# Latent attention of a decoder kernel: absorbed rank weights by three products per head pair, with the moved rows made by transfers on chip

## The chip, the cores and the metric

One NeuronCore of a Trainium2 chip runs the whole program; the other cores are idle. The metric is the device time of one execution in microseconds (us), the median of several runs. The engines are TensorE (PE in the rows; PEld is its weight load), VectorE (DVE), ScalarE (ACT), GpSimd (POOL) and SyncE (SP), which issues most of the transfers (DMAs); ScalarE issues some too. Each engine works through its own instructions in order, and they wait for one another by semaphores.

## The reference

Two decoder layers on x of 4 x 256 tokens by 256, all in float32: attention with low-rank updates, latent cross attention, a quantised feed forward, attention with position bias, grouped cross attention, and a mixture of experts. The change is in the latent attention:

```python
q_hk = (hidden_q @ Wq.T).reshape(B, S, H, K)         
q_big = einsum('bshk,hkq->bshq', q_hk, w_kc_q)          # 192 per head
q_big = q_big * cos + rotate_half(q_big) * sin
kv_r = rope(kv_c)                                       # context, 64 wide
q_r = einsum('bshq,hqr->bhsr', q_big, W_qr)             # rank 64
k_r = einsum('bld,hdr->bhlr', kv_r, W_kr)
attn = softmax(einsum('bhsr,bhlr->bhsl', q_r, k_r))
ctx_lat = einsum('bhsd,hkd->bhsk', einsum('bhsl,bld->bhsd', attn, kv_r), w_kc_kv)
x = x + ctx_lat.reshape(B, S, H * K) @ Wo.T
```

`rotate_half` takes the two halves (96 each) of a head's 192 columns, swaps them and changes one's sign.

## The kernel before

`build_program` runs the stages one after another; `mla_stage` is the latent attention. It works through 8 pairs of heads p; each head has 192 query columns, so a pair has 384, three tiles of 128: tile 0 is head 0's first 128, tile 1 holds head 0's last 64 and head 1's first 64 (the shared tile), tile 2 is head 1's last 128. Tokens are worked in two halves of 512.

Instead of making k_r, the kernel absorbs both rank weights into one matrix per head, W_qr times W_kr transposed (192 x 64), so that the queries come out 64 wide and meet the rotated context directly. The queries are multiplied by the cosine and the sine table; the swap of halves is done in the weights: for the sine product, the absorbed matrix is needed with its 192 rows rolled by 96. So a pair needs the absorbed weights in two row orders. For the shared tile they are needed per head, cosine's 64 rows and sine's 64 rows stacked in one matrix of 128 rows.

One pair passes through these steps, named by the functions that issue them:

- `load_k` (L1027) brings pair p's two rank weights from memory: `wkr_in` and `wr_in`; `load_a` and `load_n` bring the others. SyncE issues them a pair ahead, behind a wait for `turned`.
- `turn(p)` (L1495): TensorE transposes `wr_in` (three tiles) and `wkr_in` into bank 5. It waits for `w_k`, the landing of `load_k`.
- `turned_weights(p)` (L1370): ScalarE copies them out, in five activations. Three write `wrT`, which has six slots of 128 columns: besides the three tiles also the rolled row orders. Two write `wkrT`, with each head's block beside zeros which GpSimd has put there (L1175).
- `absorb(p, bank)` (L1506): TensorE makes six products of 128x64, three in the cosine order and three in the sine order.
- `absorbed_weights(p, bank)` (L1225): VectorE copies the six (384 columns) to `wr`, and counts `wr_done`.
- `packed(p, k)` (L1518), k = 0 to 5: the query products, six products of 512 columns each, for half k // 3 and one tile; `rotate` on VectorE multiplies them by the tables into `qcs`.
- `scored_shared` and `scored_own` (L1540, L1552): the absorbed weights times `qcs`, per half; the first needs `wr_done`. ScalarE and VectorE split the result into a high part and a rest (`query_high`, `query_rest`), and SyncE copies the high part to `q2` (`copy_queries`).
- `scores(p, k)`, k = 0 to 7; `maximum`, `denominators`, `logarithms`, `shifts`; `shift_transpose`, `shift_rows` and `send_shifts`, a small transfer of the softmax's shifts to `q2` which `scores_t` (the transposed scores) waits for; `exponentials`; `product`; `context_high` and `context_rest`; `project` and `add`.

The order on each engine is written out by hand. TensorE, per pair: packed 2, `turn(p + 1)`, packed 3, shared products of half 0, packed 4, output weight, own products of half 0, packed 5, `fold(p + 1)`, shared products of half 1, scores 0 to 3, own products of half 1, `absorb(p + 1)`, score 4, the shifts' transpose, scores 5 to 7, transposed scores 0 and 1, packed 0 of the next pair, products, and so on; the last pair's `project` steps lie between the next pair's packed groups. VectorE's `absorbed_weights(p + 1)` stands between `query_rest(p, 1, 1)` and `maximum(p, 4)`. Score 4 waits for `query_rest(p, 1, 0)`, score 5 for `query_rest(p, 1, 1)`.

Before the pairs, TensorE does `fold(0)`, `turn(0)`, two turns of x, `absorb(0)`, two more turns of x, packed 0 and 1 of pair 0 and the transposes of the context. Packed 0 waits there for `wr_done`, since the six products lie in its bank. SyncE issues four loads of the context, and then, pair by pair:

```python
for p in range(PAIRS):
    if p + 1 < PAIRS:
        sp.wait_ge(turned.sem, turned.at(p + 1))
        c.mla.load_k(sp, p + 1)
        sp.wait_ge(folded.sem, p + 1)
        c.mla.load_a(sp, p + 1)
    ...
    sp.wait_ge(mt.sem, 2 * p + 1)
    send_shifts(sp, 0, 1)
```

Of the kernel before, what the change touches and what calls it, by code (L numbers as in the profile page):

```python
# [15 lines left out]
F32 = mybir.dt.float32  # L16
# [3 lines left out]
ALU = mybir.AluOpType  # L20
# [3 lines left out]
P = 128  # L24
# [1017 lines left out]
def mla_stage(c):  # L1042
    nc, io = c.nc, c.io
    with ExitStack() as st:
# [9 lines left out]
        wrT, wkrT = sb("wrT", [P, 6, P]), sb("wkrT", [P, 2 * CTX])  # L1054
        wr = sb("wr", [P, 2, 2, 3, R])
# [25 lines left out]
        zeroed, tern = c.counter("at_m5"), c.counter("at_m4")  # L1081
# [16 lines left out]
        EV = 5  # L1098
        TILE_ORDER = (1, 0, 2)
        WR_SLOTS = ((0, 2), (1, 4), (5, 3))  # L1100
# [28 lines left out]
        with nc.Block() as block:  # L1129

            @block.sync
            def _(sp):
# [12 lines left out]

                src = io["ctx"].rearrange("(t p) d -> p t d", p=P)
# [3 lines left out]
                sp.dma_start(tabk, io["rope_k"].rearrange("p k t d -> p k (t d)")).then_inc(ctx_in.sem, 16)  # L1150
                for p in range(PAIRS):
                    if p + 1 < PAIRS:
                        sp.wait_ge(turned.sem, turned.at(p + 1))
# [3 lines that stand above are left out]
                    if p == 0:  # L1157
                        copy_keys()
                    copy_queries(p, 0)
                    if p + 1 < PAIRS:  # L1160
                        sp.wait_ge(n_done.sem, p + 1)
                        c.mla.load_n(sp, p + 1)
                    copy_queries(p, 1)
                    sp.wait_ge(mt.sem, 2 * p + 1)
                    send_shifts(sp, 0, 1)

            @block.gpsimd
            def _(pool):
# [6 lines left out]
                pool.memset(wkrT[:, :], 0.0).then_inc(zeroed.sem, 1)  # L1175
                pool.wait_ge(zeroed.sem, zeroed.at(1))
                pool.memset(kLt[CTX:CTX + 2, :].bitcast(F32), 1.0).then_inc(zeroed.sem, 1)
                pool.wait_ge(zeroed.sem, zeroed.at(2))
# [21 lines left out]
            def _(dve):  # L1200
# [24 lines left out]
                def absorbed_weights(p, bank):  # L1225
                    dve.wait_ge(absorbed.sem, p + 1)
                    dve.tensor_scalar(wr[:, p % 2, :, :, :].rearrange("p j t n -> p (j t n)"),  # L1227
                                      c.ps[:, bank, 0:6 * R], 1.0, None, ALU.mult).then_inc(wr_done.sem, 1)
# [136 lines left out]
            def _(act):  # L1365
# [4 lines left out]
                def turned_weights(p):  # L1370
                    act.wait_ge(turned.sem, turned.at(p + 1))
                    ps = c.ps[:, TURN_BANK, :]
                    dst = wrT[:, :, :].rearrange("p t n -> p (t n)")
                    act.activation(dst.rearrange("p (k n) -> p k n", n=DCQ)[:, 0:4:3, :],
                                   ps[:, 0:2 * DCQ].rearrange("p (h n) -> p h n", h=2), ACT.Copy)\
                        .then_inc(turned_ev.sem, 1)
                    act.activation(dst[:, DCQ:DCQ + 448].rearrange("p (h n) -> p h n", h=2)[:, :, 0:160],
                                   ps[:, 32:352].rearrange("p (h n) -> p h n", h=2), ACT.Copy).then_inc(turned_ev.sem, 1)
                    act.activation(dst[:, 352:416].rearrange("p (h n) -> p h n", h=2),
                                   ps[:, 0:2 * DCQ].rearrange("p (k n) -> p k n", n=32)[:, 0:12:11, :], ACT.Copy)\  # L1380
                        .then_inc(turned_ev.sem, 1)
                    for h in range(2):
                        act.activation(wkrT[rows(h), h * CTX:(h + 1) * CTX], ps[rows(h), 3 * P:3 * P + CTX], ACT.Copy)\
                            .then_inc(turned_ev.sem, 1)
# [62 lines left out]
                act.wait_ge(zeroed.sem, zeroed.at(2))  # L1447
# [34 lines left out]
            def _(pe):  # L1482
# [23 lines left out]
                def absorb(p, bank):  # L1506
                    pe.wait_ge(turned_ev.sem, turned_ev.at(EV * p + EV))
                    if p:
                        pe.wait_ge(mp_lo.sem, p + 1)
                    for j in range(2):  # L1510
                        for tile in range(3):
                            h = (0, j, 1)[tile]
                            mm = pe.matmul(c.ps[:, bank, (3 * j + tile) * R:(3 * j + tile + 1) * R],
                                           wrT[:, WR_SLOTS[tile][j], :], wkrT[:, rows(h)],
                                           start=True, stop=True)
                    mm.then_inc(absorbed.sem, 1)
# [23 lines left out]
                def scored_shared(p, half):  # L1540
                    pe.wait_ge(rope.sem, rotated(p, 3 * half + 1))
                    if half == 0:
                        pe.wait_ge(wr_done.sem, p + 1)
# [4 lines left out]
                    for h in range(2):  # L1548
                        pe.matmul(c.ps[rows(h), 4 + half, :], wr[:, p % 2, h, 1, :], qcs[:, half, 1, h, :],
                                  start=True, stop=False, skip_group_check=True)  # L1550

                def scored_own(p, half):  # L1552
                    pe.wait_ge(rope.sem, rotated(p, 3 * half + 3))
                    for cs in range(2):
                        for h, tile in ((0, 0), (1, 2)):
                            mm = pe.matmul(c.ps[rows(h), 4 + half, :], wr[:, p % 2, cs, tile, :],
# [39 lines left out]
                def scores_t(p, b):  # L1596
# [3 lines left out]
                    if b == 0:  # L1600
                        pe.wait_ge(mt.sem, 2 * p + 1)
                        pe.wait_ge(q_lo.sem, 4 * p + 4)
                        if p == 0:
                            pe.wait_ge(zeroed.sem, zeroed.at(2))
# [113 lines left out]
        for s, n in ((stats_done, TT), (mv_done, TT), (var_done, 2), (std_done, 2), (rstd_done, 2),  # L1718
# [3 lines left out]
                     (zeroed, 2)):  # L1722
# [1535 lines left out]
```

## Time and profile before

| | us |
|---|---|
| median of 3 runs | 812.61 (811.94 to 814.03) |
| profiled execution, its span | 812.5 |

| engine | busy us in the span | share |
|---|---|---|
| PE | 722.5 | 89% |
| DVE | 577.6 | 71% |
| PEld | 462.7 | 57% |
| ACT | 425.3 | 52% |
| POOL | 198.0 | 24% |

The latent attention takes about 111 to 414 us of the span. Busy shares are means over stages with different limits, so each step is read from the timeline of its own stretch. A matmul's end is modelled and overlaps the next one's start; "idle before" is what the engine lay idle ahead of an instruction, and the name behind the arrow is who ended it; "issue" means that nothing in the profile shows the wait. SPq and ACTq rows are a queue's issuing of transfers, not the transfers themselves.

### The profile page before, as it was taken

How to read it: one execution, taken by the hardware profiler on the slowest of the kernel's cores; microseconds unless marked ns; L12 is line 12 of the kernel's file. 1: busy time of each engine (PE TensorE's matmuls, PEld its weight loads, DVE VectorE, ACT ScalarE, POOL GpSimd, SP SyncE). 2: the span in 40 equal slices, each digit the busy share in tenths (PEclk: the TensorE clock that was granted, in tenths of full speed). 3: DMA queues.
4: the chain of work that ended last, by engine and by line, in shares of the span. 5: the costliest groups of instructions: out<-in, count | busy, mean ns of one | idle time of the engine just before them, and what ended most of it. 6: DMA issues, size and time to landing. Idle time of an engine off the chain costs nothing. (4 is left out here: it accounts for less than half of the span.)

```text
span 812.5 us, 13314 instructions
## 1 busy us (share of the span) xinstructions
PE 722.5 (89%) x4826; PEld 462.7 (57%) x4826; DVE 577.6 (71%) x1117; ACT 425.3 (52%) x888; POOL 198.0 (24%) x298
## 2 busy tenths in 40 slices
PE   5999989999999999999757469999589999879997
PEld 3555666666666666666533345666344444368886
DVE  5578678686767667686669854565668999665666
ACT  4557753544636364543649655455366676533332
POOL 2422010303123030303225314120121111352450
PEclk9999999999999999999979679999859999969999
DMA  4725422111202111110153006130010323403111
GB/s 120 194 60 158 148 70 69 48 45 34 76 7 72 30 49 36 42 43 1 27 135 75 9 8 191 45 80 2 21 41 21 81 59 90 120 2 106 54 50 52
DMA packets 49760, 52.24 MB, mean 64 GB/s; under 512 B 10116, under 2 KB 40388, under 8 KB 49588
## 3 DMA queue, kind: packets, MB, share of 16 engines
q1 hardware_dynamic: 49062, 51.06, 23.4%
q8 instruction: 39, 0.64, 0.3%
q10 hardware_dynamic: 634, 0.33, 0.2%
q14 instruction: 25, 0.20, 0.1%
HBM read 26.58 MB, written 2.04 MB: 35 GB/s over the span
## 5 line engine op out<-in xcount | busy, mean ns | idle before, releaser
L427 DVE TENSOR_REDUCE a_nm<-ps 128x2 f32<-128x512 f32 (+1 forms) x112 | 75.3, 688 | 28.4 <-PE ps L723 19.4
L2499 DVE TENSOR_REDUCE x_nm<-ps 128x2 f32<-128x512 f32 x128 | 84.9, 685 | 12.4 <-PE ps L2640 10.1
L2584 ACT ACTIVATE x_pt<-ps 128x1024 f32<-128x1024 f32 x64 | 62.4, 1020 | 34.6 <-PE ps L2668 33.9
L1535 PE MATMUL ps<-m_xp,m_mp 128*128 128x512 f32 x288 | 75.4, 397 | 1.0 <-DVE m_wr L1227 1.0
L1406 ACT ACTIVATE m_junk<-ps,m_nm 128x256 bf16<-128x256 f32 x128 | 58.6, 483 | 25.8 <-DVE m_nm L1244 25.8
L1191 POOL TENSOR_SCALAR fw<-fw,finv 128x256 f32<-128x256 f32 x24 | 11.6, 482 | 223.7 <-PE ps L1613 223.7
L2640 PE MATMUL ps<-kx,a_qs 96*128 96x256 bf16 x256 | 53.1, 296 | 8.2 <-DMA a_qs<-a_ks 6.5
L1535 PEld LDWEIGHTS ps<-m_xp,m_mp 128*128 128x128 f32 x288 | 50.7, 188 | 15.4 <-issue 6.1
L3068 PE MATMUL ps<-x_xp,x_wp 128*128 128x512 f32 x216 | 55.2, 407 | 0.0
L1207 DVE TENSOR_TENSOR m_qcs<-ps,mw_tab 64x512 f32<-64x512 f32 x64 | 44.0, 688 | 7.5 <-PE ps L1535 4.3
L1214 DVE TENSOR_TENSOR m_qcs<-ps,mw_tab 128x512 f32<-128x512 f32 x64 | 41.1, 684 | 7.4 <-PE ps L1535 7.1
L3068 PEld LDWEIGHTS ps<-x_xp,x_wp 128*128 128x128 f32 x216 | 41.2, 196 | 8.6
L2640 PEld LDWEIGHTS ps<-kx,a_qs 96*128 96x128 bf16 x256 | 20.6, 101 | 41.2 <-issue 13.2
L2684 PE MATMUL ps<-x_pt,a_ks 128*32 128x256 f32 x512 | 41.8, 399 | 2.6 <-DVE x_av L2508 2.6
L1244 DVE TENSOR_REDUCE m_nm<-ps 128x2 f32<-128x512 f32 x64 | 39.8, 680 | 1.0 <-PE ps L1574 1.0
L1574 PE MATMUL ps<-m_kHH,m_qs 128*128 128x256 f32 x128 | 33.9, 302 | 6.8 <-DVE m_qs L1237 4.4
L2668 PE MATMUL ps<-a_qs,kx 98*128 98x512 bf16 x128 | 39.6, 392 | 0.0
L1426 ACT ACTIVATE m_pt<-ps 128x1024 f32<-128x1024 f32 x32 | 31.0, 1017 | 14.1 <-PE ps L1613 14.1
L575 ACT ACTIVATE a_pt<-ps 128x1024 f32<-128x1024 f32 x32 | 32.1, 1019 | 10.6 <-PE ps L758 10.6
L575 ACT ACTIVATE fw<-ps 128x1024 f32<-128x1024 f32 (+1 forms) x32 | 25.8, 810 | 22.0 <-PE ps L774 21.9
L1629 PE MATMUL ps<-m_pt,m_kvr 128*64 128x256 f32 x256 | 33.4, 391 | 1.8 <-ACT m_pt L1426 1.4
L1574 PEld LDWEIGHTS ps<-m_kHH,m_qs 128*128 128x128 f32 x128 | 24.9, 194 | 16.2 <-issue 7.3
(306 smaller groups left out, 1673.8 us busy)
## 6 DMA issues: line engine op xcount, KB each, us to landing
a_qs<-a_parts SPq DMA_DIRECT2D x48, 128.0 KB
a_ks<-a_parts SPq DMA_DIRECT2D x48, 128.0 KB
m_q<-m_qs SPq DMA_DIRECT2D x32, 128.0 KB
x_gb<-scr_g SPq DMA_DIRECT2D x8, 512.0 KB, 3.8
fw<-in_f_w SPq DMA_DIRECT2D x12, 256.0 KB
a_qs<-a_ks SPq DMA_DIRECT2D x48, 64.0 KB
mw_wq<-in_m_wq SPq DMA_DIRECT2D x8, 256.0 KB, 2.8
mw_wo<-in_m_wo SPq DMA_DIRECT2D x8, 256.0 KB, 2.8
```

Source lines behind the costliest of these rows:

```text
L427: dve.tensor_reduce(dst, src, AX.X, ALU.max, negate=True).then_inc(mx_done.sem, 1)
L575: act.activation(pt[:, n % 2, kt, 0:banks * BANK], c.ps[:, 2 + 2 * kt:2 + 2 * kt + banks, :].rearrange("p b n -> p (b n)"), ACT.Exp, scale ...
L1207: dve.tensor_tensor(qcs[rows((cs, 1 - cs)[h]), half, 1, h, :].rearrange("p (b q) -> p b q", q=SEQ), c.ps[rows(h), QB_BANKS[k], :].rearrang ...
L1214: dve.tensor_tensor(qcs[:, half, tile, cs, :].rearrange("p (b q) -> p b q", q=SEQ), c.ps[:, QB_BANKS[k], :].rearrange("p (b q) -> p b q", ...
L1406: act.activation(junk[:, n % 4, :], c.ps[:, S_BANKS[k % 4], qt * SEQ:(qt + 1) * SEQ], ACT.Exp, bias=nm[:, k // 4, one], accum_out=den[:, k ...
L1535: mm = pe.matmul(c.ps[:, QB_BANKS[k], :], mp[:, p % 2, w, dt, tile * P:(tile + 1) * P], xp[:, x, dt, half_cols(half)], start=((dt, w, x) = ...
L1574: mm = pe.matmul(c.ps[:, S_BANKS[k % 4], qt * SEQ:(qt + 1) * SEQ], qs[:, h, q0:q0 + P], part[:, seq_cols(b)], start=(low == 0), stop=(low ...
L2499: dve.tensor_reduce(nm[:, n % ITEMS, QT * u:QT * u + QT], c.ps[:, u % 2, :].rearrange("p (t k) -> p t k", t=QT), AX.X, ALU.max, negate=Tru ...
L2584: act.activation(pt[:, n % 2, kt, :], c.ps[:, 2 + 2 * kt:4 + 2 * kt, :].rearrange("p b n -> p (b n)"), ACT.Exp, scale=SCALE).then_inc(exp_ ...
L2640: mm = pe.matmul(c.ps[:, u % 2, qt * SEQ:(qt + 1) * SEQ], queries(slice(0, S_ROWS), n, u).squeeze(1)[:, qt * P:(qt + 1) * P], kx[0:S_ROWS, ...
L2684: mm = pe.matmul(c.ps[rows(h), 6, 0:SEQ], vs[:, QT * b + kt, g, :], pt[:, n % 2, kt, h * SEQ:(h + 1) * SEQ], start=(kt == 0), stop=(kt == ...
L3068: mm = pe.matmul(up_bank(j, half), wp[:, b, w, at:at + EH], xp[:, x, dt, cols(half)], start=((dt, w, x) == terms[0]), stop=((dt, w, x) == ...
```

## The change

The rank weights are absorbed once, in the cosine order only: `wrT` has three tiles, copied in one piece; `wkrT` has 64 columns, copied in one piece, and no zeros (the other head's part is zero in `wr_in` itself). Three products per pair take the place of six, and VectorE copies 192 columns. The rows of the other order, and the stacked rows of the shared tile, are moved from `wr` to a new tile `wm` by ten transfers per pair, of 32 or 64 rows with 256 bytes each, which SyncE issues behind a wait for `wr_done`: for pair 0 ahead of its pair loop, for pair p + 1 at the end of pair p. The shared products wait for the ten transfers (`wm_in`) in place of `wr_done`. GpSimd's memset of `wkrT` goes.

```diff
-        wrT, wkrT = sb("wrT", [P, 6, P]), sb("wkrT", [P, 2 * CTX])
-        wr = sb("wr", [P, 2, 2, 3, R])
+        wrT, wkrT = sb("wrT", [P, 3, P]), sb("wkrT", [P, CTX])
+        wr, wm = sb("wr", [P, 2, 3, R]), sb("wm", [P, 2, 4, R])
...
-        EV = 5
+        EV = 2
         TILE_ORDER = (1, 0, 2)
-        WR_SLOTS = ((0, 2), (1, 4), (5, 3))
+        MOVES = ((0, 0, 0, 96, 32), (0, 32, 1, 0, 64), (0, 96, 0, 0, 32),
+                 (1, 0, 1, 0, 64), (1, 64, 0, 32, 64), (2, 0, 2, 32, 64), (2, 64, 1, 64, 64),
+                 (3, 0, 2, 96, 32), (3, 32, 1, 64, 64), (3, 96, 2, 0, 32))
...
+                def move_weights(p):
+
+                    sp.wait_ge(wr_done.sem, p + 1)
+                    for to, row, tile, first, count in MOVES:
+                        sp.dma_start(wm[row:row + count, p % 2, to, :], wr[first:first + count, p % 2, tile, :])\
+                            .then_inc(wm_in.sem, 16)
+
...
                 sp.dma_start(tabk, io["rope_k"].rearrange("p k t d -> p k (t d)")).then_inc(ctx_in.sem, 16)
+                move_weights(0)
                 for p in range(PAIRS):
...
                     send_shifts(sp, 0, 1)
+                    if p + 1 < PAIRS:
+                        move_weights(p + 1)
...
-                pool.memset(wkrT[:, :], 0.0).then_inc(zeroed.sem, 1)
+                pool.memset(kLt[CTX:CTX + 2, :].bitcast(F32), 1.0).then_inc(zeroed.sem, 1)
                 pool.wait_ge(zeroed.sem, zeroed.at(1))
-                pool.memset(kLt[CTX:CTX + 2, :].bitcast(F32), 1.0).then_inc(zeroed.sem, 1)
-                pool.wait_ge(zeroed.sem, zeroed.at(2))
...
-                    dve.tensor_scalar(wr[:, p % 2, :, :, :].rearrange("p j t n -> p (j t n)"),
-                                      c.ps[:, bank, 0:6 * R], 1.0, None, ALU.mult).then_inc(wr_done.sem, 1)
+                    dve.tensor_scalar(wr[:, p % 2, :, :].rearrange("p t n -> p (t n)"),
+                                      c.ps[:, bank, 0:3 * R], 1.0, None, ALU.mult).then_inc(wr_done.sem, 1)
...
+                    act.activation(wrT[:, :, :].rearrange("p t n -> p (t n)"), c.ps[:, TURN_BANK, 0:3 * P], ACT.Copy)\
                         .then_inc(turned_ev.sem, 1)
...
+                    act.activation(wkrT[:, :], c.ps[:, TURN_BANK, 3 * P:3 * P + CTX], ACT.Copy)\
                         .then_inc(turned_ev.sem, 1)
...
-                    for j in range(2):
-                        for tile in range(3):
-                            h = (0, j, 1)[tile]
-                            mm = pe.matmul(c.ps[:, bank, (3 * j + tile) * R:(3 * j + tile + 1) * R],
-                                           wrT[:, WR_SLOTS[tile][j], :], wkrT[:, rows(h)],
-                                           start=True, stop=True)
+                    for tile in range(3):
+                        mm = pe.matmul(c.ps[:, bank, tile * R:(tile + 1) * R], wrT[:, tile, :], wkrT[:, :],
+                                       start=True, stop=True)
...
                     if half == 0:
-                        pe.wait_ge(wr_done.sem, p + 1)
+                        pe.wait_ge(wm_in.sem, wm_in.at(16 * len(MOVES) * (p + 1)))
...
-                        pe.matmul(c.ps[rows(h), 4 + half, :], wr[:, p % 2, h, 1, :], qcs[:, half, 1, h, :],
+                        pe.matmul(c.ps[rows(h), 4 + half, :], wm[:, p % 2, 1 + h, :], qcs[:, half, 1, h, :],
...
-                            mm = pe.matmul(c.ps[rows(h), 4 + half, :], wr[:, p % 2, cs, tile, :],
+                            w = wm[:, p % 2, 3 * h, :] if cs else wr[:, p % 2, tile, :]
+                            mm = pe.matmul(c.ps[rows(h), 4 + half, :], w,
```

## Rows read from the trace of the kernel before

**Rows 1.** Windows of about a pair: TensorE's busy us come first, its clock after POOL
```profile
126.00:161.00 35.00, 33.47 (x182) 21.32 (x180) 27.10 (x48) 17.76 (x54) 7.23 (x9) 1.00 0.27 68
...
232.00:268.00 36.00, 34.60 (x195) 22.75 (x194) 25.78 (x47) 17.74 (x54) 7.20 (x9) 1.00 0.16 44
```

**Rows 2.** Timeline of TensorE in pair 2: start, duration, engine, line, operation
```profile
213.58 1.55 PE L1513 MATMUL ps<-m_wkrT,m_wrT 128*128 128x64 f32 x12
215.24 0.36 PE L1574 MATMUL ps<-m_kHH,m_qs 128*128 128x256 f32 x1
...
216.69 0.35 PE L1574 MATMUL ps<-m_kHH,m_qs 128*128 128x256 f32 x1 [0.55 <-DVE m_qs L1237]
...
218.72 0.47 PE L1612 MATMUL ps<-m_qs,m_kHH 128*128 128x512 f32 x1 [0.39 <-issue]
...
222.72 2.23 PE L1629 MATMUL ps<-m_pt,m_kvr 128*64 128x256 f32 x16
...
232.82 0.49 PE L1502 MATMUL ps<-ident,mw_wr_in 128*128 128x128 f32 x3
```

**Rows 3.** Timeline of VectorE in the same pair
```profile
204.26 0.41 DVE L1262 TENSOR_TENSOR m_wn<-ps,m_wn 128x256 fp32r<-128x256 f32 x1
...
209.62 0.96 DVE L1222 TENSOR_TENSOR m_mp<-ps,m_mp 128x768 fp32r<-128x768 f32 x1
...
214.41 0.68 DVE L1237 TENSOR_TENSOR m_qs<-ps,m_qs 64x512 fp32r<-64x512 f32 x1
...
216.57 0.56 DVE L1227 TENSOR_SCALAR m_wr<-ps 128x384 f32<-128x384 f32 x1
```

**Rows 4.** Timeline of ScalarE in the same pair
```profile
217.76 0.47 ACT L1406 ACTIVATE m_junk<-ps,m_nm 128x256 bf16<-128x256 f32 x1 [1.32 <-DVE m_nm L1244]
...
221.66 1.92 ACT L1426 ACTIVATE m_pt<-ps 128x1024 f32<-128x1024 f32 x2
...
239.72 0.38 ACT L1388 ACTIVATE m_wn<-ps 128x256 fp32r<-128x256 f32 x1 [4.91 <-PE ps L1593]
```

**Rows 5.** Timeline of all engines at the start of the stage
```profile
115.23 1.00 SPq L1029 DMA_DIRECT2D mw_wr_in<-in_m_wr  x1
...
120.18 0.55 DVE L1227 TENSOR_SCALAR m_wr<-ps 128x384 f32<-128x384 f32 x1
...
122.17 1.30 POOL L1184 TENSOR_TENSOR m_kvr<-m_qcs 128x512 f32<-128x512 f32 x1
...
125.96 0.49 PE L1502 MATMUL ps<-ident,mw_wr_in 128*128 128x128 f32 x3
```

**Rows 6.** Issues by line: ns of one issue, min/median/max, first and last start
```profile
L1136 SPq DMA_DIRECT2D m_q<-m_qs x32: 461/468/511, 133.8 to 395.4; - x32
...
L1126 SPq DMA_DIRECT2D m_q<-m_mT x8: 687/691/692, 144.0 to 396.0; - x8
...
L1024 SPq DMA_DIRECT2D mw_wq<-in_m_wq x8: 429/430/433, 92.9 to 327.4; - x8
```

**Rows 7.** Issues of the keys' load, and the rank load's time from issue to landing
```profile
L1028 SPq DMA_DIRECT2D mw_wkr_in<-in_m_wkr x8: 529/710/734, 93.8 to 326.0; - x8
...
DMA to landing us min/median/max: 2.5/2.6/5.4
```

**Rows 8.** Windows around two falls of TensorE's clock, columns as in rows 1
```profile
392.20:395.70 3.50, 1.69 (x9) 0.62 (x5) 2.48 (x7) 3.09 (x14) 0.00 (x0) 0.98 0.17 37
395.70:399.10 3.40, 2.89 (x13) 2.92 (x14) 2.44 (x4) 2.21 (x10) 0.00 (x0) 0.51 0.18 41
...
473.90:477.50 3.60, 0.00 (x0) 0.00 (x0) 3.02 (x10) 0.00 (x0) 2.65 (x1) 1.00 0.05 1
...
479.30:487.70 8.40, 7.67 (x15) 3.74 (x16) 3.81 (x15) 6.86 (x17) 0.00 (x0) 0.50 0.02 4
```

**Rows 9.** ScalarE's shifts of the second half, and the transposed scores behind them
```profile
223.75 1.28 ACTq L1126 DMA_DIRECT2D m_q<-m_mT  x2
...
226.37 0.39 PE L1612 MATMUL ps<-m_qs,m_kHH 128*128 128x512 f32 x1
```

More of the change, by code:

```diff
@@ L1080, in mla_stage @@
         xp_hi, xp_lo = c.counter("at_in3"), c.counter("at_in4")
-        zeroed, tern = c.counter("at_m5"), c.counter("at_m4")
+        zeroed, tern, wm_in = c.counter("at_m5"), c.counter("at_m4"), c.counter("at_m6")
         w_a, w_k, w_n, tab_in = c.mla.w_a, c.mla.w_k, c.mla.w_n, c.mla.tab_in
@@ L1371, in turned_weights @@
                     act.wait_ge(turned.sem, turned.at(p + 1))
[L1372 to L1375, printed above, removed]
+                    act.activation(wrT[:, :, :].rearrange("p t n -> p (t n)"), c.ps[:, TURN_BANK, 0:3 * P], ACT.Copy)\
                         .then_inc(turned_ev.sem, 1)
[L1377 to L1380, printed above, removed]
+                    act.activation(wkrT[:, :], c.ps[:, TURN_BANK, 3 * P:3 * P + CTX], ACT.Copy)\
                         .then_inc(turned_ev.sem, 1)
-                    for h in range(2):
-                        act.activation(wkrT[rows(h), h * CTX:(h + 1) * CTX], ps[rows(h), 3 * P:3 * P + CTX], ACT.Copy)\
-                            .then_inc(turned_ev.sem, 1)
                 def weight_high(p):
@@ L1446, in _ @@
                 fold_high(0)
-                act.wait_ge(zeroed.sem, zeroed.at(2))
                 turned_weights(0)
@@ L1603, in scores_t @@
                         if p == 0:
-                            pe.wait_ge(zeroed.sem, zeroed.at(2))
+                            pe.wait_ge(zeroed.sem, zeroed.at(1))
                     if b == 1:
@@ L1721, in mla_stage @@
                      (dn, 16 * PAIRS), (ln_done, 2 * PAIRS), (ms, 6 * PAIRS), (wn_lo, PAIRS), (tern, 9 * PAIRS),
-                     (zeroed, 2)):
+                     (zeroed, 1), (wm_in, 16 * len(MOVES) * PAIRS)):
             s.done(n)
```

## The prediction

> **What bounds the kernel now.** I read, in this order: the page's busy shares and slices, the windows of one head pair each, the timelines of TensorE, VectorE, ScalarE and SyncE over one steady pair, and the first 30 us of the latent attention stage. The change touches that stage alone (about 111 to 414 us of the span of 812.5). A pair takes 36 us and TensorE is busy 34.6 of them [rows 1], so TensorE looks like the bound. The timeline says more: inside a pair there is a stretch, from the products that finish the queries' second half to the first context products, where TensorE waits for others. Score 4 starts at 215.24, right after VectorE's query rest, which runs 0.68 from 214.41 and ends at 215.09; the next score starts after an idle 0.55, put down to VectorE; the transposed scores start after 0.39 [rows 2, 3]. There the order is ScalarE's and VectorE's: maxima, eight denominators, a logarithm, exponentials. In pair 0 TensorE has hardly a gap (33.47 busy of 35.00) [rows 1], so there whatever holds it up for long is paid.
>
> **TensorE: three products fewer per pair.** The six products take 1.55 from 213.58 [rows 2]; half is 0.78. But score 4 can't start before 215.09 (the rest) plus some 0.1, and the six end at 215.13. So TensorE would now wait for VectorE where it multiplied: worth 0, in all seven pairs that do it there. If VectorE's query parts were faster, this would be worth up to 0.78 a pair. For pair 0's own weights TensorE next waits for normalised rows, also 0.
>
> **ScalarE: two copies for five.** Two stay, one of 128x384 and one of 128x64. After the five ScalarE idles 4.91 for the output weight [rows 4]. Worth 0.
>
> **VectorE: 192 columns copied, not 384.** The copy takes 0.56; 128x256 takes 0.41 and 128x768 0.96, about 1.07 ns a column, so 192 fewer save 0.2 [rows 3]. The maximum behind it starts 0.2 earlier, and ScalarE, which had waited 1.32 for that maximum, starts its eight denominators 0.2 earlier; they, a logarithm and the exponential at 221.66 run without a pause, and the context products at 222.72 wait for that exponential [rows 2, 4]. TensorE's own queue before those products leaves some 0.1 of that uncertain, because the transposed scores at 218.72 wait for something else, the shifts' transfer. I take 0.17 a pair: 7 x 0.17 = 1.2 gained, between 0.7 and 1.4.
>
> **GpSimd: one memset fewer.** It then waits for normalised rows anyway; its last product starts at 122.17 and ends at 123.47, and the key transposes wait for that. So the 0.2 that VectorE's shorter copy gives the first packed products of pair 0 is stopped there too. Worth 0 [rows 5].
>
> **SyncE: ten transfers per pair, and what they are put ahead of.** In pairs 0 to 6 they follow SyncE's last transfer of the pair: from about 217.2, behind the copy, to 222.3 at 0.51 each (below). Behind them stand the loads for the pair after next, which land by about 227 and are turned at 232.82 [rows 2]; the moved weights are read after that turn. Worth 0, apart from a collision, below.
>
> Before pair 0 it is otherwise. SyncE now waits for the copy of the absorbed weights (VectorE, from 120.18, now 0.35 long, so 120.53), issues ten transfers, and only then loads pair 1's rank weights, which it had issued at 115.23 [rows 5]. Pair 1's turn is the next thing that TensorE does after the third packed group, at 125.96, and TensorE takes its queue in order: packed groups, scores and all stand behind it. How long does one issue take? The nearest row is the on-chip copy of 64 rows of the queries: 468 ns, with 0.04 between two; bounds are 430 (a load of 128 rows) and 691 (the shifts, few rows) [rows 6]. Sum: 120.53 + 0.05 + 10 x 0.51 = 125.7; the keys' load 0.71 + 0.04, so the rank load is issued at 126.45; it lands 2.6 later [rows 7], 129.05, and the turn's products start at about 129.25, where they had started at 125.96. **Cost 3.3**; with 430 it is 2.9, with 691 it is 5.1, and a slower landing (up to 5.4 is seen) would add. Pair 0 has no slack on TensorE to give it back, and all later pairs follow it.
>
> One sentence of the Trainium skill bears on that price: DMA: Bandwidth & Descriptors, section "Why a DMA increments its semaphore by 16 and not by 1", gives 512 sequencer cycles per transfer on earlier generations, and TensorE: Matmul & The Clock Gate, Part 1, a sequencer at 1.2 GHz, which is 0.43 us. The loads' row agrees (430), the on-chip copy's doesn't (468); by the page the forecast would be 815.6.
>
> **The clock in that hole.** TensorE would be idle for 3.3 us at 125.9. In the trace it lay idle from 473.9; the granted clock was 1.00 until 477.5 and 0.50 from there, and the engine then worked through 8.4 us (479.3 to 487.7) at that level, 1.2 GHz. Less idle time did it too: in pair 7 the engine was busy 1.69 of 3.50 from 392.2, and the clock was 0.51 from 395.7 to 399.1 [rows 8]. So I take it that the hole costs a fall. Work of 3.4 us at half rate loses 1.7; 8.4 us would lose 4.1; none loses 0. I take 1.8, nearer the first, since the queue behind the hole is dense as in that stretch.
>
> **Sum**, against the profiled 812.5 (its median of runs is 812.61, so 0.1 is added): +3.3 +1.8 -1.2 = +3.9, **816.4**.
>
> **Rivals.**
> (a) The clock doesn't fall in the hole: 812.6 + 3.3 - 1.2 = 814.7. For it: where a gap lies seems to matter, since after the idle start at 473.9 it took 3.6 us to fall. Against: pair 7, with less idle. 20%.
> (b) The four loads for the next pair but one, moved some 5 us back by the transfers, now fly when ScalarE sends the shifts of the second half. Those are issued from 223.75 for 1.28, and the transposed scores start at 226.37 with no wait, 2.0 after the second issue; so there may be little slack [rows 9]. Loads beside them could add 0.3, in six pairs: +1.8, 818.2. Landing times of the rank load itself go from 2.5 to 5.4 with what else is in flight [rows 7]. 18%. 
> (c) Not slower: the six products are on the path after all. Place: ahead of score 4. Price: 0.78 x 7 = 5.4 gained, 816.4 - 5.4 = 811.0. It decides if score 4 waits for TensorE's queue and not for the query rest, that is if the rest is done before 214.4. Against: it ends at 215.09 and score 4 follows it by 0.15. 7%.
> (d) The new 0.8 us gap ahead of score 4, beside those of 0.55 and 0.39, lets the clock fall in the steady pairs as in pair 7. There 3.4 us went at 0.51, which costs up to 1.7; in half of the seven pairs that is +6.0, 822.4. Against: the three gaps sum to 1.7 over more than 4 us, where pair 7 had 1.81 idle in 3.50. 7%.
> Some 3% is left for what I don't see; the forecast has 45%.
>
> **Range and chances.** Low end: (a) with issue at its cheapest and all of VectorE's gain, 812.6 + 2.9 - 1.4 = 814.1, less 0.2 for runs. High end: issue at 691 and 2.6 for the clock, 812.6 + 5.1 + 2.6 - 0.7 = 819.6, which also holds (b); (c), (d) and part of the last 3% lie outside, under 2 in 10. 0.3% is 2.4 us, about what a measurement of this kernel can tell from no change, so slower means above 815.0: nearly all of the forecast, all of (b) and (d), a quarter of (a): 0.77. Same: the rest of (a) and a little of (c): 0.17. Faster: most of (c): 0.06.
>
> **What would show it.** In the profile of the changed kernel: TensorE idle for about 3.3 us ahead of pair 1's turn, released by the rank load; SyncE's ten issues in a row at about 0.5 each from 120.6; granted clock 0.5 soon after; in a steady pair a wait of about 0.8 ahead of score 4 put down to VectorE's query rest, the copy of the absorbed weights at 0.35, a pair shorter by 0.1 to 0.2. Wrong if pair 1's turn isn't held up, if an issue takes well under 0.4, or if steady pairs are shorter by 0.7 or longer than before.

## The result and the profile after

The changed kernel took 819.05 us in the median of four runs (817.93 to 820.97), beside 813.31 for the kernel before in the same session: ratio 1.0073, 95% interval 1.0053 to 1.0092. Measured once more in six runs it gave 820.19 beside 813.41, ratio 1.0073 (1.0052 to 1.0095). So it is slower, by 5.7 to 6.8 us. The profiled execution has a span of 819.2 against 812.5.

The page of the changed kernel, its head (busy us, share of the span, instructions; then the DMA packets):

```profile
span 819.2 us, 13272 instructions
PE 722.8 (88%) x4778; PEld 463.2 (57%) x4778; DVE 577.5 (70%) x1117; ACT 420.3 (51%) x864; POOL 197.9 (24%) x297
...
DMA packets 55137, 53.30 MB, mean 65 GB/s; under 512 B 15492, under 2 KB 45764, under 8 KB 54964
```

TensorE executes 48 matmul instructions fewer and is busy no less (722.5 before). ScalarE is busy 5.0 less; copy_ahead (experiment 4) has ScalarE's two copies too, and its pairs take what they took before, so nothing came of it.

**Where the time is.** A good ruler is VectorE's copy of the absorbed weights, which starts once in each pair. Its starts in the changed kernel (the first to the fourth, and the eighth), then the second, third, and eighth of the kernel before (the first and fourth stand in [rows 5] and [rows 3]):

```profile
120.05 0.34 DVE L1237 TENSOR_SCALAR m_wr<-ps 128x192 f32<-128x192 f32 x1
150.72 0.36 DVE L1237 TENSOR_SCALAR m_wr<-ps 128x192 f32<-128x192 f32 x1
186.80 0.36 DVE L1237 TENSOR_SCALAR m_wr<-ps 128x192 f32<-128x192 f32 x1
223.23 0.36 DVE L1237 TENSOR_SCALAR m_wr<-ps 128x192 f32<-128x192 f32 x1
...
367.44 0.36 DVE L1237 TENSOR_SCALAR m_wr<-ps 128x192 f32<-128x192 f32 x1
```

```profile
144.09 0.56 DVE L1227 TENSOR_SCALAR m_wr<-ps 128x384 f32<-128x384 f32 x1
180.33 0.56 DVE L1227 TENSOR_SCALAR m_wr<-ps 128x384 f32<-128x384 f32 x1
361.60 0.56 DVE L1227 TENSOR_SCALAR m_wr<-ps 128x384 f32<-128x384 f32 x1
```

First interval: 30.67 against 23.91, so +6.76. The six steady ones: 216.72 against 217.51 together, so -0.79; five of them are 36.03 to 36.08 where before they were 36.24 to 36.27, and one is 36.43. Nearly the whole loss is made between the start of the stage and the second pair's weights. Ahead of the first copy the two traces differ by 0.13, behind the eighth by 0.86.

Timeline of SyncE, then of TensorE, at the start of the stage in the changed kernel (start, duration, engine, line; in brackets idle time and what ended it):

```profile
120.42 6.31 SPq L1152 DMA_DIRECT2D m_wm<-m_wr  x10
126.77 0.59 SPq L1028 DMA_DIRECT2D mw_wkr_in<-in_m_wkr  x1
127.41 0.59 SPq L1029 DMA_DIRECT2D mw_wr_in<-in_m_wr  x1
```

```profile
120.54 3.88 PE L1532 MATMUL ps<-m_xp,m_mp 128*128 128x512 f32 x12 [0.24 <-DVE m_wr L1237]
...
125.04 1.63 PE L1532 MATMUL ps<-m_xp,m_mp 128*128 128x512 f32 x6
130.13 0.90 PE L1502 MATMUL ps<-ident,mw_wr_in 128*128 128x128 f32 x3 [3.45 <-DMA mw_wr_in<-in_m_wr]
130.96 0.37 PE L1503 MATMUL ps<-ident,mw_wkr_in 64*128 64x64 f32 x1
131.26 2.93 PE L1532 MATMUL ps<-m_xp,m_mp 128*128 128x512 f32 x6
```

And windows of the same stretch (busy us of PE, PEld, DVE, ACT, POOL, then TensorE's clock, DMA share, GB/s):

```profile
119.00:123.00 4.00, 3.76 (x12) 2.91 (x13) 2.66 (x5) 2.48 (x3) 3.81 (x3) 0.57 0.04 9
123.00:127.00 4.00, 3.68 (x21) 2.76 (x19) 3.68 (x6) 1.02 (x1) 0.00 (x1) 1.00 0.11 24
127.00:129.00 2.00, 0.00 (x0) 0.00 (x0) 2.00 (x3) 0.00 (x0) 0.00 (x0) 1.00 0.24 47
129.00:136.00 7.00, 5.87 (x14) 2.80 (x14) 2.39 (x5) 0.60 (x2) 0.00 (x0) 0.52 0.69 201
```

The ten moves go first, the rank load behind them is issued at 127.41 and lands for the turn at 130.13; TensorE stands idle for 3.45 with everything queued behind the turn, and then works 7 us at a clock of 0.52 (1.2 GHz of 2.4): six packed products take 2.93, which take 1.67 or less at the full clock.

From the first copy to the turn it is 10.08 us, against 5.78 before [rows 5]: +4.30. From the turn to the second copy it is 20.59 against 18.13: +2.46. That is the 6.76.

### The profile page after: what moved, and what is told of

The parts are those of the page before. It is cut to its first block and busy times, and to the rows that moved or that the text cites. A ratio compares the mean times of both kernels' runs of the same rounds, so it can differ in the third digit from the quotient of the medians.

```text
span 819.2 us, 13272 instructions
## 1 busy us (share of the span) xinstructions
PE 722.8 (88%) x4778; PEld 463.2 (57%) x4778; DVE 577.5 (70%) x1117; ACT 420.3 (51%) x864; POOL 197.9 (24%) x297
## 5 line engine op out<-in xcount | busy, mean ns | idle before, releaser
L1532 PE MATMUL ps<-m_xp,m_mp 128*128 128x512 f32 x288 | 77.5, 406 | 0.2 <-DVE m_wr L1237 0.2
L1532 PEld LDWEIGHTS ps<-m_xp,m_mp 128*128 128x128 f32 x288 | 52.4, 193 | 15.7 <-issue 4.8
```

Of the source, the lines that this page charges most:

```text
L1532: mm = pe.matmul(c.ps[:, QB_BANKS[k], :], mp[:, p % 2, w, dt, tile * P:(tile + 1) * P], xp[:, x, dt, half_cols(half)], start=((dt, w, x) = ...
```

## The experiments

All of them are timed beside the kernel before, whose median was 813.2 to 813.4 each time. "Interval" below is from one start of the copy of the absorbed weights to the next.

**1. The place of the rank load.** In loads_first SyncE issues pair 1's four loads ahead of pair 0's moves:

```
+                sp.wait_ge(turned.sem, turned.at(1))
+                c.mla.load_k(sp, 1)
+                sp.wait_ge(folded.sem, 1)
+                c.mla.load_a(sp, 1)
                 move_weights(0)
                 for p in range(PAIRS):
-                    if p + 1 < PAIRS:
+                    if 0 < p and p + 1 < PAIRS:
```

> The changed kernel with one difference: SyncE issues pair 1's four loads ahead of pair 0's ten transfers, as soon as pair 0's turn is done. Theory (the rank load stood behind the transfers, and TensorE, in order, behind the load): pair 1's turn starts at about 125.5 to 126.5, not 130.1; the shared products may now wait up to 1 for the last transfer; from VectorE's first copy of absorbed weights to its second 24 to 25 us, not 30.7; the time is 812 to 813.5. Rival (the ten transfers as such, or the shared products' new wait for them, cost the time, wherever they are issued): first interval over 28, time 817 or more.

Measured: 813.6 us (10 runs, 811.69 to 816.51), ratio 1.0007 (0.9991 to 1.0022). TensorE at the start of the stage:

```profile
119.23 5.05 PE L1536 MATMUL ps<-m_xp,m_mp 128*128 128x512 f32 x12 [0.23 <-DVE m_wr L1241]
...
126.40 0.49 PE L1506 MATMUL ps<-ident,mw_wr_in 128*128 128x128 f32 x3
126.82 0.27 PE L1507 MATMUL ps<-ident,mw_wkr_in 64*128 64x64 f32 x1
127.02 1.65 PE L1536 MATMUL ps<-m_xp,m_mp 128*128 128x512 f32 x6
128.60 1.08 PE L1550 MATMUL ps<-m_qcs,m_wm 128*64 128x512 f32 x4
```

The turn waits for nothing, nor do the products at 128.60 that read the moved weights, whose last move was issued 3 us before. One reordering gives back the whole loss, so the place of the load is its cause, and the ten moves as such cost nothing here. But the first interval is 25.54, not below the 23.91 of before: the first twelve packed products took 5.05, where they take 2.97 to 2.99 at the full clock. That is taken up in 3. The six later intervals are 36.24, 36.37, 36.06, 36.42, 36.15 and 36.06; the clock fell in the fourth of them only.

five_five puts pair 1's four loads (the four lines added above) between the first five moves and the last five:

```
+                move_weights(0, MOVES[:5])
...
+                move_weights(0, MOVES[5:])
```

> The changed kernel with five of pair 0's ten transfers issued ahead of pair 1's four loads and five behind them. Theory (the hole is the queue's issue time, 0.63 us a transfer): the rank load is issued 3.1 us earlier, at about 124.3, lands at about 127, TensorE waits 0.5 to 1.0 for it, the clock does not fall there, the first interval is about 25, and the time is 813 to 814.5. Rival (a fixed cost of waiting for the copied weights, whatever the count): a wait of TensorE of over 2.5 remains and the time stays above 816.

Measured: 814.74 us (10 runs), ratio 1.0012 (1.0000 to 1.0024), first interval 25.78. The rank load was issued at 122.28, the turn ran at 125.70, with no wait (I had expected 0.5 to 1.0; the low clock ahead of it, with twelve products in 5.00, brought TensorE there later):

```profile
125.70 0.49 PE L1507 MATMUL ps<-ident,mw_wr_in 128*128 128x128 f32 x3
```

Half the moves ahead of the load cost 1.1 at most (814.74 against 813.6, and the intervals of the two ratios overlap), all ten cost the turn 4.3: the price is not so much per move, it begins where the load's landing passes TensorE's arrival at the turn.

**2. The clock behind the hole.** hole_filled keeps the changed kernel's order and gives TensorE 14 unused products to make where it would stand idle; hole_half gives it 8; their results are overwritten.

```
+                    if p == 0:
+                        pe.wait_ge(xp_lo.sem, xp_lo.at(4))
+                        for _ in range(14):
+                            pe.matmul(c.ps[:, 4, :], mp[:, 0, 0, 0, 0:P], xp[:, 0, 0, half_cols(0)],
+                                      start=True, stop=True)
                     if p + 1 < PAIRS:
                         turn(p + 1)
```

> The changed kernel with 14 products more (128x512, their result is not used) on TensorE ahead of pair 1's turn, where it lay idle for the rank load. Theory (behind the hole the granted clock was 0.50 for 6.7 us, and that costs time on top of the wait): the turn still starts at about 130, the clock stays 1.00 from 126 to 136, the first interval is about 28.3, not 30.7, and the time falls by 2 to 2.5. Rival (what follows the hole is limited by VectorE or by transfers, and the clock is only a sign): the clock stays 1.00 but the first interval stays above 30 and the time within 0.5 of 819.

> hole_filled once more, for a second profile: its first one showed a first interval of 28.48 with the clock at 1.00 behind the hole, yet its timed runs lie at 821. Theory: in some executions the low clock that begins at about 117 lasts into the 14 added products; at half rate they take 6 us instead of 3.3 and reach past the landing of the load, so that the span is 819 and the first interval about 31. Rival: the profile is as the first one (span about 816), and the timed runs are later for another reason.

> The changed kernel with 8 products more ahead of pair 1's turn instead of 14: at half rate they take 3.4 us and still end before the load lands. Theory (the low clock behind the hole costs about 2.2): where the clock stays up the first interval is about 28.5, where it falls 30.7; the turn starts at 130 either way; median 816.5 to 819, below the changed kernel's 819.05, never clearly above it. Rival (the clock behind the hole costs nothing): median 819 to 820.

TensorE in hole_filled, and its window behind the hole:

```profile
126.23 3.34 PE L1677 MATMUL ps<-m_xp,m_mp 128*128 128x512 f32 x14
129.41 0.49 PE L1502 MATMUL ps<-ident,mw_wr_in 128*128 128x128 f32 x3
...
130.03 1.66 PE L1532 MATMUL ps<-m_xp,m_mp 128*128 128x512 f32 x6
```

```profile
129.00:136.00 7.00, 7.00 (x33) 3.74 (x33) 4.15 (x7) 0.99 (x3) 0.00 (x0) 1.00 0.57 149
```

And in hole_half, where 1.60 of idle time was left:

```profile
126.29 2.00 PE L1677 MATMUL ps<-m_xp,m_mp 128*128 128x512 f32 x8
129.89 0.55 PE L1502 MATMUL ps<-ident,mw_wr_in 128*128 128x128 f32 x3 [1.60 <-DMA mw_wr_in<-in_m_wr]
```

The first interval came to 28.48, 28.71 and 27.97, with the clock at 1.00 behind the hole in all three. From the turn to the second copy they need 17.93, 17.91 and 17.94, alike; the kernel before needs 18.13, the changed one 20.59. So in the profiles the wait alone is worth 4.3 and the clock 2.7. The 0.2 between 18.13 and 17.93 is not VectorE's shorter copy, which lies ahead of the turn. It goes with a late turn: loads_first and loads_ahead (5), whose turn comes 7.7 behind the first copy, need 17.88 and 17.89, while the kernels of 3 and 4 with the turn 5.6 to 5.8 behind it need 18.06 to 18.13, with the short copy or the long one. Only five_five (7.6 and 18.19) doesn't fit. So pair 0 gives back 0.2 of the hole; what work it is that has got ahead by then isn't shown. The profile of hole_filled_2 is also where I was wrong: I had expected the added products to run at half rate; they ran at the full one.

The medians follow this badly. hole_filled took 821.0 (818.02, 821.0, 821.01, 821.68; the profiled one is the fastest; ratio 1.0096, 1.0071 to 1.0120), where I had expected 2 to 2.5 less than 819.05; hole_filled_2 took 820.28 in its one run, hole_half 818.63 (four runs, ratio 1.0062, 1.0039 to 1.0085), where 819.05 less 2.7 would have been 816.4. Two losses can be named. The 14 products hold up the turn themselves: it comes 10.55 and 10.80 behind the first copy, not 10.08 (with 8 products 10.03). And in hole_filled_2 the second interval is 37.15, with a low clock from 148 to 151. These don't make up the difference, and the rest isn't explained. To see whether the changed kernel's fall itself is there only in some runs, it ran once more:

> The changed kernel once more, unedited. Its first profile was that of its slowest run (820.97), with TensorE's clock at 0.5 for 6.7 us behind the hole and a first interval of 30.67; the kernels with products added in the hole had 28.0 to 28.7 at full clock, but were not faster in the median (818.6 and 821.0 against 819.05). Theory (the fall behind the hole is there in every run): first interval 30.5 to 30.8 again, median 819 to 820. Rival (it comes in some runs only, and the first profile caught one of them): first interval near 28.3 with the clock at 1.00 behind the hole, or a median under 818.5.

First interval 30.51, median 820.19, and the low clock lay in the same places: from 118, 128, 186, 367 and 401, where the first profile has 119, 129, 187, 368 and 402. The fall behind the hole was in both profiles of the changed kernel. But that falls keep their places in every run isn't shown: hole_filled and hole_filled_2 are one kernel, and the low clock begins at 116, 256 and 399 in the one, at 117, 147, 185, 366 and 400 in the other. (The Trainium skill, TensorE: Matmul & The Clock Gate, "What's actually happening", says of a kernel's start that the number of products at the low clock varies from run to run. The two profiles of hole_filled vary in that way, though in the middle of a kernel; the two of the changed kernel don't.) What keeping the fall away is worth in the time stays open: 2.7 in three profiles of the stretch, nothing that the medians of four runs can show.

**3. Three products fewer.** six_products is loads_first with each of the three products made twice, so that TensorE has its six again (the second three are never read); VectorE copies 192 columns. six_in_pair_0 does so for pair 0 alone (its range is 6 for pair 0 and 3 for the others).

```
-                    for tile in range(3):
+                    for tile in range(6):
-                        mm = pe.matmul(c.ps[:, bank, tile * R:(tile + 1) * R], wrT[:, tile, :], wkrT[:, :],
+                        mm = pe.matmul(c.ps[:, bank, tile * R:(tile + 1) * R], wrT[:, tile % 3, :], wkrT[:, :],
```

> loads_first with the three products of each pair made twice (six, the second three into columns that nobody reads); VectorE still copies 192 columns. Theory (TensorE's three products fewer are worth nothing, because score 4 waits for VectorE's query rest): score 4 starts as long after the own products as in loads_first, a steady pair takes 36.05 in both, and the time is that of loads_first within 0.5, or below it if the filled gap spares falls of the clock. Rival (the products are on the path): 0.7 to 0.8 a pair more, 36.8, and 5 us more in all.

> loads_first with the three products of pair 0's weights made twice, the other pairs' once. Theory (with three products fewer between the two halves of x TensorE idles longer there, 1.15 instead of 0.48, and the clock falls at about 117, which costs about 1.6 at the packed groups): no low clock before 125, first interval 23.6 to 23.9 as in six_products; steady pairs still show one to three falls; time 1 to 1.5 below loads_first's 813.6. Rival (that fall comes with the place of the loads, not with the products): low clock at 117 to 124 as before, first interval 25.5.

six_products: 812.67 us (10 runs), ratio 0.9989 (0.9975 to 1.0003), intervals 23.66 and then 36.06 to 36.12. six_in_pair_0: 814.2 (10 runs), ratio 1.0012 (0.9995 to 1.0029), intervals 23.66, then 36.05 to 36.11 with two of 36.41 and 36.45. The steady pair is 36.05 to 36.1 with six products, and three don't shorten it: the six steady intervals together are 216.53 in six_products and 216.80 in six_ahead (5), and 216.72 to 217.43 in the kernels with three, hole_filled_2 with its 218.21 left aside. So the three products fewer gain nothing there. And the three that are missing in pair 0 do harm. Timeline of TensorE ahead of the first packed products and windows of that stretch, first in loads_first:

```profile
114.78 0.78 PE L1515 MATMUL ps<-m_wkrT,m_wrT 128*128 128x64 f32 x6
116.71 2.30 PE L1656 MATMUL ps<-ident,xn 128*128 128x128 f32 x8 [1.15 <-DVE xn L1306]
```

```profile
117.00:124.00 7.00, 6.77 (x20) 5.09 (x20) 5.04 (x10) 2.48 (x3) 3.82 (x3) 0.52 0.12 35
```

then in six_in_pair_0:

```profile
115.26 1.45 PE L1515 MATMUL ps<-m_wkrT,m_wrT 128*128 128x64 f32 x12
117.19 1.73 PE L1656 MATMUL ps<-ident,xn 128*128 128x128 f32 x8 [0.48 <-DVE xn L1306]
119.72 2.97 PE L1536 MATMUL ps<-m_xp,m_mp 128*128 128x512 f32 x12 [0.79 <-DVE m_wr L1241]
```

```profile
117.00:124.00 7.00, 6.02 (x31) 4.61 (x32) 5.42 (x12) 2.77 (x4) 3.83 (x3) 1.00 0.14 45
```

With 0.67 us less work TensorE stands idle for 1.15, not 0.48, and then works 7 us at 0.52 of its clock; the first interval is 25.54 instead of 23.66. In the changed kernel the same fall begins at 119 (twelve products in 3.88 instead of 2.97), but it is hidden there, since the turn waits for the load, which doesn't hang on TensorE. In the time this 1.9 too is not to be seen: I had expected 1 to 1.5 less than loads_first, and six_in_pair_0 is no faster in the median (814.2 and 813.6, the intervals overlap). Its profile has four stretches of 3.4 at the low clock in the stage (from 179, 288, 360, 394), that of loads_first has two behind the start (253, 396); and from the eighth copy to the end of the span the one needs 451.3, the other 448.8. That the clock takes at one place what it gives at another isn't shown by this.

One thing is shown by all the profiles together. Nine of them have three products in the steady pairs (the changed kernel's two, loads_first, five_five, hole_filled's two, hole_half, six_in_pair_0, loads_ahead), and in each the clock falls one to three times behind the second to eighth copy, 18 falls in all, every one beginning within 1 us of the start of a copy: right behind the new wait of 0.8 ahead of score 4 and the 0.55 ahead of score 5 that was there before. The five with six products (before, six_products, six_and_copy, copy_ahead, six_ahead) have none in that stretch. So it is the three missing products that let the clock fall in steady pairs too. Such an interval takes 36.37 to 36.45, once 37.15 (the second interval of hole_filled_2). In the changed kernel:

```profile
187.00:191.00 4.00, 4.00 (x17) 3.67 (x18) 2.83 (x5) 3.21 (x15) 0.00 (x0) 0.57 0.21 47
```

**4. VectorE's copy, and a collision.** six_and_copy is six_products with VectorE copying 384 columns again (the last 192 are never read), meant to measure the copy alone.

```
-                    dve.tensor_scalar(wr[:, p % 2, 0:3, :].rearrange("p t n -> p (t n)"),
-                                      c.ps[:, bank, 0:3 * R], 1.0, None, ALU.mult).then_inc(wr_done.sem, 1)
+                    dve.tensor_scalar(wr[:, p % 2, 0:6, :].rearrange("p t n -> p (t n)"),
+                                      c.ps[:, bank, 0:6 * R], 1.0, None, ALU.mult).then_inc(wr_done.sem, 1)
```

> six_products with VectorE copying all 384 columns: apart from the transfers it does the kernel before's work. Theory (VectorE's shorter copy is what shortens a pair, by 0.17 to 0.2): steady pairs 36.25 instead of 36.06 to 36.12, time 1.0 to 1.4 above six_products, that is level with the kernel before, so that the ten transfers of the steady pairs cost nothing. Rival (the transfers cost something that the shorter copy has hidden): pairs above 36.3 and time above 814.5.

Measured: 817.02 us (6 runs), ratio 1.0047 (1.0029 to 1.0065), intervals 23.88, then 37.12, 37.24, 37.29, 37.28, 36.27, 37.02: about a whole microsecond more in five pairs of six, for 0.2 of VectorE, with no low clock in them. Timeline of a steady pair:

```profile
224.48 0.59 SPq L1028 DMA_DIRECT2D mw_wkr_in<-in_m_wkr  x1
224.52 1.32 ACTq L1128 DMA_DIRECT2D m_q<-m_mT  x2
225.12 0.59 SPq L1029 DMA_DIRECT2D mw_wr_in<-in_m_wr  x1
...
228.10 0.47 PE L1614 MATMUL ps<-m_qs,m_kHH 128*128 128x512 f32 x1 [0.78 <-issue]
```

ScalarE's two shifts leave at the very moment of SyncE's loads, and the transposed scores, which wait for the shifts, start late. In six_products the loads are issued at 222.07 and the shifts at 221.91, just ahead of them, and there is no such wait. Nor is there in the one pair of six_and_copy that takes 36.27: there the shifts go out at 299.10, the loads at 299.25, and the scores start at 301.72, 2.62 behind the shifts. If that is the cause, the loads have only to be moved. copy_ahead is the same kernel, with each pair's four loads ahead of its moves:

```
                     send_shifts(sp, 0, 1)
+                    if p + 2 < PAIRS:
+                        sp.wait_ge(turned.sem, turned.at(p + 2))
+                        c.mla.load_k(sp, p + 2)
+                        sp.wait_ge(folded.sem, p + 2)
+                        c.mla.load_a(sp, p + 2)
                     if p + 1 < PAIRS:
                         move_weights(p + 1)
```

> This is six_and_copy (three products made twice, copy of 384 columns) with one thing moved: in every pair SyncE issues the four loads for the pair after next ahead of the ten moves, not behind them. Theory (the loads' transfers, issued at the same moment as ScalarE's shifts, held these back): the transposed scores start with no wait of 0.8, the steady pairs go from 37.1-37.3 back to 36.2-36.3, the span from 814.8 to about 808 to 809.5 if no clock fall comes, 811 in the median. Rival (VectorE's longer copy is what costs 1.0 per pair): pairs stay at 37.1-37.3, the time at 817.

Measured: 813.45 us (12 runs), ratio 1.0004 (0.9994 to 1.0014), intervals 23.85, then 36.24 to 36.27 all six. The same place:

```profile
223.29 1.28 ACTq L1128 DMA_DIRECT2D m_q<-m_mT  x2
...
225.91 0.40 PE L1614 MATMUL ps<-m_qs,m_kHH 128*128 128x512 f32 x1
```

From the shifts' issue to the scores: 3.58 us beside the loads, 2.62 without them. So the collision is real and costs 0.8 to 1.0 a pair; and moves that are being issued at that moment, as here (ten from 219.10 for 6.5), cost nothing in this kernel. copy_ahead and six_products together also price VectorE's 192 columns: 36.25 with them (as in the kernel before), 36.05 to 36.1 without; and from the first copy to the turn 5.78 with them, 5.58 without. The time fell by 3.6, less than the 6 that I had written: the eight copies lie closer by 4.7 (246.1 to 241.4), and behind the eighth 1.0 was lost again.

**5. The change without its faults.** loads_ahead is the changed kernel with the order of copy_ahead, six_ahead the same with each product made twice.

> The changed kernel with the loads of every pair ahead of its moves (the best form of the change that keeps three products). Theory: as loads_first, first interval 25.5, steady pairs 36.05 or 36.4 where the clock falls in one, 813.6 in the median, level with before. Rival (rival b of the prediction was at work in small in the changed kernel): pairs 0.1 to 0.3 shorter than in loads_first, time 812 or less.

> six_products (three products made twice, copy of 192 columns) with the loads ahead of the moves in every pair. Theory: no collision was left to remove there (its transposed scores waited 0.2 at most), so pairs stay at 36.05 to 36.1, and the time within 1 of 812.7. Rival (the loads behind the moves cost something in every pair that I don't see): pairs fall to 35.9 or less, time under 811.7.

loads_ahead: 813.23 us (12 runs), ratio 1.0002 (0.9992 to 1.0013), intervals 25.62, then 36.08 to 36.41. six_ahead: 812.56 (12 runs), ratio 0.9985 (0.9974 to 0.9996), intervals 23.66, then 36.07 to 36.11 with one of 36.36 (no fall; the transposed scores came 2.82 behind the shifts there, and why isn't shown). So the best of the forms tried here is level with the kernel before, or 0.15% faster (six_ahead; six_products alone is not clear of no change) if TensorE is kept as busy as it was: about what VectorE's shorter copies give, 7 x 0.17 = 1.2 by the prediction, of which 0.8 is seen. Neither order differs from its partner in 1 and 3 (813.6 and 812.67), so in the changed kernel no collision was at work.

## Why the prediction was right, and where its sizes were off

It said 816.4, slower, in 813.9 to 819.6; it was 819.05, and 820.19 when it was measured again, which is 0.6 above the range. The mechanism and its place were right (1). The two larger terms were too small, by 1.0 and 0.9, and a fall in a steady pair (+0.4, rival (d)) was left out of the sum; so the range held by little.

- **The wait for the rank load, +3.3.** Measured +4.30. The failing step is the price of an issue: I took 0.51 from the copy of 64 rows of the queries [rows 6], with the 0.04 between two, and bounded it by 691 ns. The moves' rows are 575, 595 and 1141 ns (least, median, most, 80 of them) with 0.04 between two, 0.63 together:

```profile
L1152 SPq DMA_DIRECT2D m_wm<-m_wr x80: 575/595/1141, 120.4 to 373.9; - x80
```

  Ten take 6.35 instead of 5.1. The landing (130.13 - 127.41 = 2.72) was as taken. The truth lay about halfway between the two rows; I had chosen near the cheaper end. (The Trainium skill's 512 cycles per transfer, DMA: Bandwidth & Descriptors, section "Why a DMA increments its semaphore by 16 and not by 1", misses these rows by more: 0.43 for 0.595. The loads of `wq` agree with it, 430; the rank load, also of 128 rows, took 579 to 825 in the changed kernel.) Two of the sums beside the forecast leave out the 0.04 between two issues: with it, 691 ns gives 5.5 and not 5.1, and the top of the range 820.0; and the time by the skill's figure is 816.0 and not 815.6.
- **The clock behind the hole, +1.8.** It fell, where I said. It cost 2.7 in the profiles (2), with 0.2 given back by the late turn. It stayed low for 6.7 us, nearer the longer of my two examples [rows 8] than the shorter, whose size I took. Rival (a), no fall, is out: both profiles of the changed kernel show it.
- **VectorE's shorter copy, -1.2.** Right: 36.05 against 36.25 (4). The first copy, which I had put at 0 because GpSimd would stop it, gives 0.2 as well (5.58 against 5.78 from it to the turn, in 4); in the changed kernel the hole covers that.
- **Pair 0 has no slack.** Right in what followed, since of the hole only 0.2 came back. But the rows that I read it from don't say so: TensorE is idle for 1.53 of 35.00 in pair 0 and for 1.40 of 36.00 in a steady pair [rows 1].
- **TensorE's three products, 0.** Right in the steady pairs, and so was the new wait ahead of score 4:

```profile
220.23 0.88 PE L1511 MATMUL ps<-m_wkrT,m_wrT 128*128 128x64 f32 x6
221.89 0.36 PE L1572 MATMUL ps<-m_kHH,m_qs 128*128 128x256 f32 x1 [0.78 <-DVE m_qs L1247]
```

  Rival (c) is out with it (3). For pair 0 "also 0" was wrong in kind: with the longer idle time the clock fell (3). It came out as 0 only because the hole covered it; where the hole is mended it costs 1.9 of the first interval.
- **Rival (d), the gap lowers the clock in steady pairs.** It did, and all nine profiles with three products show it (3). So 7% was too little, but the price was too high: in the changed kernel one of six intervals has a fall (36.43, clock 0.57 from 187 to 191), at 0.37 and not at up to 1.7, and a second lies behind the eighth copy, from 368. A likely reason, not tested, is that in that stretch TensorE isn't what the pair waits for, so that most of the slower products fit into its waits.
- **Rival (b), the loads beside the shifts.** Not in the changed kernel: there the shifts go out at 230.20, the loads from 230.36, and the transposed scores at 232.83 wait for nothing. As a mechanism it was right, and worth three times my 0.3; what I had missed is how close it is: with the loads issued 0.14 to 0.16 behind the shifts there was no delay, with the loads 0.04 to 0.07 ahead there was. That the order as such decides is read from the traces; no run changed it alone. (The Trainium skill, DMA: Bandwidth & Descriptors, "Queues, rings and completion order", states the turns between the rings. That ScalarE's transfer would therefore not stand behind SyncE's was my conclusion, and it didn't hold: the measurement decides.)
- **The base.** I took the profiled execution for the median run, 0.1 apart. In each run the time is its span plus 1.8, so before's span of 812.5 belongs to a run of about 814.3. The base of the sum was the median and stands (812.61, and 813.31 with one run more); but differences of spans (6.7) and of medians (5.7) are not the same thing.

Put together from the stage: 4.3 + 2.7 for the hole, -0.2 for what the late turn gives back, -1.2 for the copies, +0.4 for the fall in a pair, 6.0. That is the 5.97 of the two traces from first to eighth copy (6.03 with the second profile), where the prediction had 3.9.

## What to carry to other kernels

When a list of transfers is put into a queue, look at what stands behind it in that queue at its first turn, before the loop is in step: there the same ten issues that are free in every later pair cost 0.7% of the kernel, and a load issued before them cost nothing. Price an issue by a row of the same shape, and where there is none let the forecast sit between the bounds, not at the cheap one. Taking work off an engine that is waiting anyway gives nothing, and for TensorE it can cost its clock; small transfers that someone waits for should not leave just behind the loads of another queue.

## What was unexpected of the hardware

- A transfer between partitions of 32 or 64 rows of 256 bytes took SyncE 0.595 us to issue, more than a load of 128 rows with 256 KB (`wq`, 0.43).
- ScalarE's shifts, issued 0.04 us after a load on SyncE's queue, were waited for until 3.58 us after their issue instead of 2.62.
- A fall of TensorE's clock cost 2.7 us where the engine had a full queue (low for 6.7 us), 1.0 in the second interval of hole_filled_2 (37.15, against 36.17 in hole_filled) and 0.37 in a steady pair (low for 3.4).
- With three small groups of products fewer per pair, TensorE's clock fell in steady pairs in all of nine profiles, right behind idle times of 0.8 and 0.55; with them, in none of five.
- 0.67 us more of idle time at one place (1.15 for 0.48), ahead of a dense stretch, went with a fall of 6.7 us at its start; nothing else had been changed between those two kernels.
- The runs of a kernel measured ten times spread by 1.7 to 6.1 us, and the last 450 us of the span, which no edit touched, differed by up to 3.7 between the profiles (448.8 to 452.6), with the falls of the clock in other numbers there. A gain of 1 to 2 us in one stage's profile can't be read off medians of four.
